# Two blocks of single-pass products per period: base, experts and router as one product, scores as two row tiles, PSUM banks dealt anew

## What is computed

```
def _L0_cond_ref(x, embedding, ...):      # a 32x32 mix of the tokens for each sequence, and a bias
    out = einsum('boi,bih->boh', agg_w, x) + agg_b[:, :, None]
def _L0_attn_ref(x, Wq, Wk, Wv, Wo):      # 32 query heads, 8 key heads, 16 wide, rope, causal
    scores = jnp.einsum('bkgqd,bkmd->bkgqm', qg, k) / np.sqrt(HEAD_DIM)
    attn = softmax(where(causal, scores, -inf)); return out @ Wo
def _L0_cond2_ref(x, c, weight, ...):     # grouped convolution of 9 taps along the features
def _L0_ffn_ref(x, base_W, base_b, router_W, router_b, A, B, expert_map):
    base_out = jnp.einsum('btd,od->bto', x, base_W) + base_b
    probs = softmax(x @ router_W.T + router_b); topk_p, topk_i = top_k(probs, 8)
    h = jnp.einsum('btd,erd->bter', x, A)     # 8 experts of rank 16
    return base_out + jnp.einsum('bter,eor->bto', h * w[..., None], B) * SCALING
x = x + _L0_attn_ref(_L0_cond_ref(x, ...), ...)
x = x + _L0_ffn_ref(_L0_cond2_ref(x, ...), ...)
```

## Time and profile before

| | us |
|---|---|
| median of 3 runs | 748.32 (747.69 to 748.35) |
| the profiled execution | 748.08 |
| its span, first to last instruction | 746.1 |
| PE busy | 711.7 (95%) |
| PE weight loads busy | 628.5 (84%) |
| DVE busy | 543.9 (73%) |
| ACT busy | 272.5 (37%) |
| POOL busy | 147.6 (20%) |

### The profile page before, as it was taken

One profiled execution on the slowest core, in us unless ns is written; L12 is line 12 of the kernel. 1 busy time (PEld: TensorE's weight loads), 2 busy tenths in 40 slices (PEclk: granted clock), 3 DMA queues, 4 the chain that ended last, 5 costly groups with the idle time before them and its releaser, 6 DMA issues.

```text
span 746.1 us, 13077 instructions
## 1 busy us (share of the span) xinstructions
PE 711.7 (95%) x4478; PEld 628.5 (84%) x4510; DVE 543.9 (73%) x1424; ACT 272.5 (37%) x635; POOL 147.6 (20%) x116
## 2 busy tenths in 40 slices
PE   5879999999999999999999999999999999999985
PEld 4578888888888888888888888888889888888874
DVE  5457787777778777777877777788777777877763
ACT  4135433333443333344333323433333344333331
POOL 5232201222221122222102222210122222012211
PEclk9979999999999999999999999999999999999999
DMA  7751100111110011111100111110011111001000
GB/s 189 169 242 29 43 17 27 42 42 42 42 42 31 15 38 42 42 42 42 40 16 28 42 42 42 42 42 14 28 42 42 42 42 42 19 23 42 29 29 29
DMA packets 27392, 35.43 MB, mean 47 GB/s; under 512 B 11651, under 2 KB 13347, under 8 KB 26998
## 3 DMA queue, kind: packets, MB, share of 16 engines
q1 hardware_dynamic: 26374, 34.88, 15.1%
q10 hardware_dynamic: 864, 0.14, 0.1%
q0 software_dynamic: 144, 0.28, 0.1%
HBM read 26.36 MB, written 8.93 MB: 47 GB/s over the span
## 4 chain that ended last, share of the span: by engine, by line
PE 82%; ACT 7%; POOL 5%; DVE 3%; issue 2%; DMA 0%; POOLq 0%; SPq 0%; DVEq 0%
PE ps L375 37%; PE ps L516 11%; PE ps L545 11%; PE ps L528 8%; POOL z_lo L786 5%; ACT raw L644 4%; PE ps L552 2%; PE ps L579 2%; ACT z_hi L644 2%; PE ps L504 2%; PE ps L562 1%; PE ps L535 1%; PE ps L536 1%; PE ps L537 1%; PE ps L526 1%
## 5 line engine op out<-in xcount | busy, mean ns | idle before, releaser
L786 POOL TENSOR_TENSOR z_lo<-raw,z_hi 128x512 fp32r<-128x512 f32 x32 | 40.8, 1274 | 561.1 <-ACT z_hi L644 561.1
L545 PEld LDWEIGHTS ps<-convW,x1ph 128*128 128x128 f32 x768 | 90.6, 192 | 2.8
L545 PE MATMUL ps<-convW,x1ph 128*128 128x128 f32 x768 | 90.9, 275 | 0.0
L644 ACT ACTIVATE x1ph<-raw 32x128 f32<-32x128 f32 x256 | 78.9, 308 | 32.0 <-DVE raw L1016 29.4
L375 PE MATMUL ps<-wqkv_hi,y_hi 128*128 128x512 f32 (+1 forms) x256 | 90.5, 353 | 0.0
L375 PE MATMUL ps<-wqkv_hi,y_lo 128*128 128x512 f32 (+1 forms) x256 | 87.4, 341 | 0.0
L375 PE MATMUL ps<-wqkv_lo,y_hi 128*128 128x512 f32 (+1 forms) x256 | 87.3, 341 | 0.0
L644 ACT ACTIVATE qk_t<-ps 128x512 f32<-128x512 f32 x32 | 19.1, 598 | 177.5 <-PE ps L505 177.5
L811 DVE TENSOR_TENSOR oT_lo<-ps,oT_hi 128x512 fp32r<-128x512 f32 x32 | 22.1, 692 | 70.8 <-ACT oT_hi L644 70.8
L528 PE MATMUL ps<-qk_t 128*128 128x256 f32 x256 | 66.7, 383 | 4.4 <-issue 2.8
L723 ACT ACTIVATE raw<-raw 128x512 f32<-128x512 f32 x64 | 40.3, 630 | 76.5 <-DVE raw L985 76.5
(11 more groups left out here) (168 smaller groups left out, 1530.1 us busy)
## 6 DMA issues: line engine op xcount, KB each, us to landing
xm<-x SPq DMA_DIRECT2D x32, 256.0 KB, 2.6
xr<-x SPq DMA_DIRECT2D x32, 256.0 KB, 2.8
out<-raw SPq DMA_DIRECT2D x32, 256.0 KB, 2.0
convb<-convb_dram SPq DMA_DIRECT2D x1, 2048.0 KB, 12.2
mixb<-mixb_dram SPq DMA_DIRECT2D x1, 1792.0 KB, 8.7
raw<-L_attn_Wq SPq DMA_DIRECT2D x4, 256.0 KB, 4.0
raw<-L_attn_Wo SPq DMA_DIRECT2D x8, 128.0 KB, 4.5
raw<-L_ffn_base_W SPq DMA_DIRECT2D x1, 1024.0 KB, 5.8
```

Of the source, the lines that this page charges most:

```text
L545: last = mm(zo[:, :, b * S:(b + 1) * S], x1ph[:, b, s:s + P], convW[:, s, :, :], start=(s == 0), stop=(s == SHIFTS - 1))
L644: return nc.scalar.activation(dst, src, ACT.Copy)
L786: nc.gpsimd.tensor_tensor(z_lo[:, :, :].rearrange("p j n -> p (j n)"), zs, z_hi[:, :, :].rearrange("p j n -> p (j n)").bitcast(F32), ALU.s ...
```

## The change

TensorE's period is put in another order, with one more step of depth (t runs to 34, the loop is 4 to 30):

- `base` and `heads` become `feed_forward(t-2)`. The weights of both stand side by side (`ffn_hi`, `ffn_lo`, 512 + 144 columns), and each of the 12 pairs of operands gives a product of 384 columns to bank 6 and one of 272 to bank 7. The last 128 columns of the base product thus lie in bank 7.
- `lora` moves up, behind `keys_values`, and is for group t-3. Its last 128 columns go to bank 5: three products of 384 columns and three of 128.
- One block of one-pass products is now `queries`, `keys_values`, `lora(t-3)`, `project(t-1)`; the other is `feed_forward(t-2)`.
- `scores` works on two halves of the contraction rows: heads 0 to 3 in rows 0 to 63 go to bank 0, heads 4 to 7 in rows 64 to 127 to bank 1, eight f32 products of 64 rows and 128 columns. `kT` is half as wide (128x512).
- `conv` writes to bank 1, `mix` to bank 5, `transpose_o` to bank 3, `transpose_hw` to bank 2.
- `mix(t+1)` stands ahead of `scores(t)`. `values(t)` waits for `x1_sb` and for `ys_sb` of `mix(t+1)`, since it writes to banks 4 and 5.
- DVE adds the output in three pieces: `x1b[:, 3, :] += ` bank 7 (`last_sb`) in step t-2, and two adds into `outS` in step t-3. `zs` moves to the head of the next step, `route` behind `ys`, `route2` behind `normalize`.

```
             def values(t):
-                wait(pe, zs_sb, t)
+                wait(pe, x1_sb, t)
+                if live(t + 1):
+                    pe.wait_ge(ys_sb, t + 2)
...
-                    for b in (2 * h, 2 * h + 1):
-                        last = mm(ps[:, h, (b % 2) * 256:(b % 2) * 256 + 256], qT[:, b, :, :].rearrange("p g q -> p (g q)"),
-                                  kT[:, b, :, :].rearrange("p k m -> p (k m)"), start=False, stop=(b % 2 == 1))
-                    last.then_inc(s_ps, 1)
+                for b in range(NB):
+                    for h in range(2):
+                        rows = slice(h * P // 2, (h + 1) * P // 2)
+                        last = mm(ps[:, h, b * P:(b + 1) * P], qT[rows, b, :, :].rearrange("p g q -> p (g q)"),
+                                  kT[rows, b, :, :].rearrange("p k m -> p (k m)"), start=False, stop=(b == NB - 1))
+                        if b == NB - 1:
+                            last.then_inc(s_ps, 1)
...
+            def feed_forward(u):
+
+                pe.wait_ge(z_hi_sb, u + 1)
+                pe.wait_ge(z_lo_sb, u + 1)
+                wait(pe, out_sb, u)
                 for j in range(PH):
-                    for a, b in ((z_hi, base_hi), (z_hi, base_lo), (z_lo, base_hi)):
-                        mm(ps[:, 6, :], a[:, j, :], b[:, j, :], start=(n == 0), stop=False)
-                        n += 1
+                    for n, (a, b) in enumerate(((z_hi, ffn_hi), (z_hi, ffn_lo), (z_lo, ffn_hi))):
+                        first, final = j == 0 and n == 0, j == PH - 1 and n == 2
+                        mm(ps[:, 6, 0:BASE6], a[:, j, :], b[:, j, 0:BASE6], start=first, stop=False)
+                        last = mm(ps[:, 7, 0:P + NAR], a[:, j, :], b[:, j, BASE6:D + NAR], start=first, stop=final)
+                last.then_inc(ar_ps, 1)
...
+            def lora(u):
+
+                pe.wait_ge(hwT_hi_sb, u + 1)
+                pe.wait_ge(hwT_lo_sb, u + 1)
+                for n, (a, b) in enumerate(((hwT_hi, lora_hi), (hwT_hi, lora_lo), (hwT_lo, lora_hi))):
+                    mm(ps[:, 6, 0:BASE6], a[:, :], b[:, 0:BASE6], start=False, stop=(n == 2))
+                    last = mm(ps[:, 5, 0:P], a[:, :], b[:, BASE6:D], start=(n == 0), stop=(n == 2))
+                last.then_inc(ffn_ps, 1)
...
+                    out3 = outS.rearrange("p (n j) -> p j n", j=PH)
+                    v.tensor_tensor(out3[:, 0:3, :], ps[:, 6, 0:BASE6].rearrange("p (j n) -> p j n", j=3), x1b[:, 0:3, :], ALU.add)
+                    v.tensor_tensor(out3[:, 3, :], ps[:, 5, 0:P], x1b[:, 3, :], ALU.add).then_inc(out_sb, 1)
```

## The result

| | before | after |
|---|---|---|
| median, four runs each | 748.01 (747.67 to 748.35) | 755.71 (753.51 to 756.75) |
| the profiled execution | 748.08 | 754.74 |
| its span | 746.1 | 752.5 |
| one period | 21.60 | 21.67 |

A forecast was written before the change was run, and what follows sets the result against it. TensorE's passes, with one wait of about 0.4 us per period, were taken to bound the kernel before. With a period of 21.67 against 21.60, 748.08 + 2.1 + 3.3 gave 753.5 us, range 739 to 779.

The forecast's parts named there:

- the loop of waits: The period's chain of waits across TensorE and DVE: 19.5 us plus lora 1.19 and scores 0.98, giving 21.67.
- The new wait: Ahead of values, TensorE waits 0.97 us per period for DVE's softmax, eight copies and ys.
- The 0.60 saved in `feed_forward`: TensorE time saved against base and heads, 3.63 for 4.22 us; lies inside the wait for DVE, gains nothing.
- Overlap: In the scores, passes of different row halves run partly side by side: 0.98 us, range 0.86 to 1.74.
- turns (776 us): Rival: the scores' tiles take turns, 1.74 us, period 22.43, total 776 us; chance 0.25.
- the term X: Time of the scores' 16 passes of 128 columns on half the rows: taken as 0.98 us, range 0.86 to 1.74.
- My nine turns: Scores' 16 passes in order, only the second of one pair beside the first of the next: 0.98 us.
- a rival at 0.1 to 0.3: Extra waiting at the half/whole row change or by contention: 757 to 764 us, within the forecast's range (chance 0.48).
- the floor I gave: Lower limit for lora's 128-column products, 0.109 us each, what a weight load allows; 0.22 was taken.
- `hw`: Behind values: there 2.64 us after their end, its transpose at 2.76, about 0.1 of waiting past the convolution.
- Keys: Ahead of the scores: keys take 0.20, 0.69 and 0.23 us; mix covers 0.90, leaving 0.2 of waiting.
- Outside the loop: Beyond the per-period loop: start +1 and tail +2.3 us, beside +2.1 for about 30 periods.

The follow-up runs named there:

- a: Changed kernel with DVE's eight copies of by_phase moved from ahead of ys to behind it; 738.34 us, ratio to before 0.9865.
- d: Changed kernel with 64 idle columns added to each of feed_forward's 12 second products (336 for 272); 757.53 us, ratio 1.0131.
- f: Changed kernel with DVE's by_phase copies behind ys and also 64 idle columns in feed_forward's second products; 751.14 us, ratio 1.0039.
- b: Changed kernel with the scores alone put back to four f32 products of 256 columns on whole rows, kT 128x1024; 771.40 us, ratio 1.0304.
- c: Kernel before with only the scores as two row tiles and kT halved; 747.93 us, ratio 0.9995.
- h: Kernel before with row-tiled scores, halved kT, and hwT_hi (ACT) and hwT_lo (DVE) in the middle of the eight copies; 741.13 us, ratio 0.9898.

## Why the prediction was right

Forecast 753.5, measured 755.71, and the range 739 to 779 held it. The period came out at exactly the predicted 21.67, by terms that compensate: the mechanism was right, the agreement to the second decimal is luck. Here is the loop of waits, piece by piece, with S the start of `feed_forward`:

| piece | predicted | in the trace after |
|---|---|---|
| S to the start of `values` | 5.46 | 387.43 to 392.99: 5.56 |
| `values` | 1.74 | to 394.82: 1.83 |
| to the next queries | 3.31 | to 398.09: 3.27 |
| the 36 products | 6.91 | 6.99 |
| `lora` | 1.19 | 0.87 |
| transposes, keys, masks | 2.08 | 384.28 to 386.24: 1.96 |
| the scores | 0.98 | to 387.43: 1.19 |
| period | 21.67 | 21.67 |

In the table `lora` is three pairs of 0.29, and a start is where the row has it.

- **The new wait** was sized at 0.97. Counted in the same way, from the last transpose's turn (391.13 + 0.86 = 391.99) to 392.99, it is 1.00. The prediction said that the trace would put it down to `ys`; it put it down to ACT, and a and d show that the prediction had the cause.
- **The 0.60 saved in `feed_forward`** gains nothing, as predicted: d adds 0.38 to the same place nearly free of charge, and f shows the full price when the cover is gone.
- **Row tiles.** Overlap was right, turns (776 us) are out: 0.056 per pass. But the term X was mis-sized, 1.19 for 0.98. My nine turns were one too many (eight pairs, 0.90), and the change of rows, which the sum had at nothing and a rival at 0.1 to 0.3, costs 0.40: 0.29 in X and 0.11 in the first product behind, which is the 0.10 by which the table's first row is over. The Trainium skill, "TensorEngine Tiling (Array Packing)", Key Properties, says that changing the tiling mode drains the engine, and it gives no price; the weight loads that begin only at 386.34, 0.10 after the last mask has gone in (386.03 + 0.21 = 386.24), and not during it, agree with it. "TensorE: Matmul & The Clock Gate", Part 3, The mechanism, of the Trainium skill would start products on different row groups some 4 ns apart; the trace agrees within a pair (less than 0.01 us), but an f32 product is two passes and the pairs take turns of 0.112, so the 16 passes still take 0.90.
- **`lora`** was mis-sized the other way. I took the price of an f32 product of 128 columns, 0.22; the pairs of 384 and 128 columns stand 0.29 apart (380.84 to 381.13), of which 0.17 are the long one's. The short one costs 0.11 to 0.12, the distance of the weight loads, which had been the floor I gave. That the code before padded 143 columns to 256 was no sign that short one-pass products are dear.
- **`hw`** ends at V + 2.64 with V the end of `values` (394.82), and its transpose is at 397.55. Both as predicted.
- **Keys.** The mix has gone in by 384.82 + 0.90 = 385.72, and the first mask, which has no record, stands one mask ahead of the second, at 386.03 - 0.21 = 385.82: 0.10 us of waiting for the 0.2 predicted.
- **Outside the loop** my sum was low. PE's output transposes mark the same point of a step in both kernels; step 2 and step 31 of after, and then of before:

```profile
94.10 0.60 PE L590 MATMUL ps<-cst,raw 128*128 128x128 f32 x4
...
722.50 0.60 PE L590 MATMUL ps<-cst,raw 128*128 128x128 f32 x4
```

```profile
92.09 0.60 PE L579 MATMUL ps<-cst,raw 128*128 128x128 f32 x4
...
719.44 0.60 PE L579 MATMUL ps<-cst,raw 128*128 128x128 f32 x4
```

The start costs 2.0 (I had put 1), the 29 periods between the two rows 3.06 - 2.01 = 1.05 (2.1 over 30: before takes 21.63 a period over many, not the 21.60 of one), and the tail 30.0 against 26.7, so 3.3 (2.3). The sum is 6.4, the difference of the spans; predicted were 5.4.

At both ends TensorE's clock fell, which I had not foreseen. First the start. Step 1 has no `feed_forward`, as there is no `z` yet, so TensorE waits for the whole softmax and then for `base_lo`, copies and `ys`. After, PE in step 1, and two windows, up to the convolution and of it:

```profile
60.44 1.09 PE L564 MATMUL ps<-cst,raw 128*128 128x128 f32 x8 [3.49 <-ACT raw L742]
63.49 3.65 PE L576 MATMUL ps<-vm,raw 128*128 128x68 f32 x16 [1.96 <-DVE ys L1077]
66.94 5.28 PE L557 MATMUL ps<-convW,x1ph 128*128 128x128 f32 x24
```

```profile
60.40:66.90 6.50, 4.50 (x24) 4.29 (x25) 3.55 (x12) 1.72 (x3) 1.26 (x1) 0.60 0.00 0
66.90:72.10 5.20, 5.20 (x27) 5.20 (x27) 0.68 (x2) 0.00 (x0) 0.00 (x0) 0.52 0.00 0
```

In 66.90 to 72.10 the granted clock is 0.52, the lower level of 1.2 GHz for nearly all of it, and the 0.60 of the window ahead is 5.2 us at that level: the clock fell at about 61.7, behind the wait of 3.49 and the transposes, when the wait of 1.96 had only begun. The values' passes go in in 3.45 us (63.49 to 66.94) where the steady period has 1.83, and the convolution in 5.12 (66.94 to 72.06) where it has 2.73, together 4.0 us more. The start is only 2.0 longer in all; what it gained elsewhere I have not taken apart. In the kernel before, the longest wait at this place was 1.08 and the clock stayed at 2.4 GHz.

The tail has the same. After, from 737.50 to 741.00:

```profile
737.50:741.00 3.50, 3.06 (x11) 3.09 (x12) 0.30 (x2) 0.00 (x0) 1.55 (x1) 0.51 0.20 75
```

Here stands the last group's `feed_forward`, behind waits of 0.78 and 1.25 us. It takes 5.0 us (737.94 to 742.97) where the steady one takes 3.70, and the route and the last `lora` hang on it. That is 1.3 us, more than the 1.0 by which the tail is over the forecast. In the kernel before, the clock was at the lower level in the tail only from 744.4 on, behind TensorE's last product. The prediction had no term for the clock.

Four expectations of experiments were missed. a's was too high and b's too low, since they put the point at which ACT's copy takes over from DVE wrongly; c's left out the small copies behind `by_phase`; and h's took the 0.38 at `lora` for the whole of what could be won, with no next wait.

What stays open: the runs of after and of its relatives scatter over some 3 to 6 us, those of before over 1 to 3. The traces that I have are one each and do not say why. Nor was it tried to keep step 1 at the upper clock.

## What to carry to other kernels

When work that used to stand between two dependent steps is moved elsewhere, follow the engine that the later step waits for over the whole stretch: what it does there on behalf of others (here 1.83 us of copies, done 2.8 us before they were wanted) is now on the path. Moving it gave 0.54 us a period, where the 0.60 of work saved had given nothing. Test which of two engines ends a wait by moving one of them; the name beside a wait is an inference, and here it named the wrong engine. A short hole in one engine's rows need not be a wait either: count the products against their weight loads first. And try columns that nobody reads at the place where columns were saved: if adding them costs nothing, saving them gained nothing.

## What was new about the chip

- A one-pass product of 128 columns behind one of 384 costs 0.11 to 0.12 us, about the distance of two weight loads, and half of a plain f32 product of that size (0.22).
- f32 passes of 128 columns on two halves of the rows go in at 0.056 us each (0.90 for 16), where passes of 128 columns on all rows take 0.112. They start in pairs, less than 0.01 us apart. Their weight loads overlap too: 16 in the row 386.34 + 0.97.
- Going from whole to half rows and back cost 0.40 us in all. 0.10 of it lies ahead of the first weight load (386.24 to 386.34), and 0.11 in the first product on whole rows again (387.43 to 387.72, where 0.18 is the rule); no run varies the two ways by themselves.
- In step 1 TensorE's clock fell to 1.2 GHz behind a wait of 3.49 us, at the start of one of 1.96: 24 passes took 5.12 us instead of 2.73. In the tail it was at that level behind waits of 0.78 and 1.25, and `feed_forward` took 5.0 instead of 3.70.
